# A ViT tower on one core: the tokenizer's loops written out, the image load behind a unit's first doubling, token tiles evacuated in two slots, an earlier meeting of the engines

## What is computed

```python
x = (x - mean) / (1e-06 + std); x = x / math.sqrt(P)          # per patch and channel
x = _conv2d(x, conv1_w, conv1_b)                               # 3x3, 3 -> 64 channels
residual = x
x = gelu(_group_norm(x, gn1_g, gn1_b)); x = _conv2d(x, rconv1_w, rconv1_b)   # 3x3, 64 -> 64
x = gelu(_group_norm(x, gn2_g, gn2_b)); x = _conv2d(x, rconv2_w, rconv2_b)   # 3x3, 64 -> 64
x = residual + x
x = _conv2d(x, proj_w, proj_b, stride=P, pad=0)                # one token of 192 per patch
embeddings = x.reshape(bsz, seq_len, E) + row_emb[row_pos][None] + col_emb[col_pos][None]
```

## Time and profile before

| what | us |
|---|---|
| median of 3 runs (lowest, highest) | 1486.84 (1485.9, 1489.83) |
| the profiled execution, its run's time | 1486.23 |
| its span in the trace | 1484.4 |
| PE busy in it | 1367.0 (92%) |
| DVE, ACT, POOL busy | 1098.0, 860.0, 582.6 |
| PE's mean granted clock | 0.98 of full speed |

### The profile page before, as it was taken

How to read it: one execution, slowest core, us unless ns; L and a number is a source line. 1 busy time by engine, 2 the same in 40 slices (tenths; PEclk the granted TensorE clock), 3 DMA queues, 4 the chain that set the end, 5 groups by cost and what they waited for, 6 DMA issues and landing times. The chain is left out here.

```text
span 1484.4 us, 43767 instructions
## 1 busy us (share of the span) xinstructions
PE 1367.0 (92%) x14042; PEld 1005.5 (68%) x14042; DVE 1098.0 (74%) x4148; ACT 860.0 (58%) x2126; POOL 582.6 (39%) x1116
## 2 busy tenths in 40 slices
PE   3999988888999999999999998999999977998889
PEld 1865543334888588768977875789588867754647
DVE  4763358999888988888898888888888864545520
ACT  1333337777767776666776766676767630343451
POOL 1000035555554544455455444455454420152600
PEclk9999999999999999999999999999999988898999
DMA  7899845544555555455545554555455579300000
GB/s 209 237 270 267 242 117 160 179 123 128 147 140 134 138 139 147 119 137 146 140 118 156 136 146 104 146 147 139 123 149 139 145 219 259 79 1 1 2 0 17
DMA packets 125141, 205.78 MB, mean 139 GB/s; under 512 B 20028, under 2 KB 88188, under 8 KB 124478
## 3 DMA queue, kind: packets, MB, share of 16 engines
q1 hardware_dynamic: 124990, 203.71, 50.3%
HBM read 103.11 MB, written 20.70 MB: 83 GB/s over the span
## 5 line engine op out<-in xcount | busy, mean ns | idle before, releaser
L629 PE MATMUL rc<-sb_acts,sb_rwd 128*64 128x512 f16 x1764 | 561.5, 391 | 21.4 <-DMA sb_acts<-sb_hst 21.2
L630 PE MATMUL rc<-sb_acts,sb_rwd 128*64 128x512 f16 x1764 | 562.3, 392 | 0.0
L481 POOL TENSOR_TENSOR sb_tmp<-sb_mst,sb_half_neg 128x8 f32<-128x8 f32 x200 | 353.6, 1768 | 463.8 <-DVE sb_mst L956 463.8
L548 ACT ACTIVATE sb_f32q<-c,sb_gsh,sb_gsc 128x128 f32<-128x128 f32 x792 | 298.3, 458 | 274.5 <-POOL sb_gsh L491 274.5
L629 PE MATMUL rc<-sb_acts,sb_rwl 128*64 128x512 f16 x1176 | 362.6, 390 | 5.3 <-issue 5.3
L630 PE MATMUL rc<-sb_acts,sb_rwl 128*64 128x512 f16 x1176 | 362.0, 390 | 0.0
L720 PE MATMUL pj_st<-sb_wall_arena 128*64 128x384 f16 x1792 | 304.0, 333 | 6.6 <-DVE sb_wall_arena L975 6.6
L568 ACT ACTIVATE sb_g2f<-rc,sb_gsh,sb_gsc 128x128 f32<-128x128 f32 x784 | 297.3, 481 | 4.6 <-POOL sb_gsh L491 4.6
L724 PEld LDWEIGHTS pj_st<-sb_wall_arena 128*64 128x64 f16 x1792 | 220.9, 222 | 65.8
L724 PE MATMUL pj_st<-sb_wall_arena 128*64 128x192 f16 x1792 | 240.9, 245 | 0.0
L629 PEld LDWEIGHTS rc<-sb_acts,sb_rwd 128*64 128x64 f16 x1764 | 179.1, 110 | 84.2 <-DMA sb_acts<-sb_hst 33.2
(11 more groups left out here) (190 smaller groups left out, 1864.0 us busy)
## 6 DMA issues: line engine op xcount, KB each, us to landing
sb_acts<-sb_hst SPq DMA_DIRECT2D x792, 78.8 KB, 2.6
sb_im<-x_planes SPq DMA_DIRECT2D x202, 136.5 KB
sb_wall_arena<-w_lo SPq DMA_DIRECT2D x48, 528.0 KB, 3.8
sb_acts<-sb_hst SPq DMA_DIRECT2D x96, 162.0 KB, 3.2
sb_wall_arena<-w_lo SPq DMA_DIRECT2D x24, 480.0 KB, 3.7
sb_f32q<-in_proj SPq DMA_DIRECT2D x12, 576.0 KB, 4.6
sb_wall_arena<-in_proj SPq DMA_DIRECT2D x12, 576.0 KB, 4.6
w_lo<-sb_wall_arena SPq DMA_DIRECT2D x8, 768.0 KB, 3.7
```

The costliest lines, as they stand in the source:

```text
L481: ch.did(gp.tensor_tensor(t1, var, half_neg[:, :], ALU.pow))
L548: ins = nc.scalar.activation(g1f[:, q * Q + m, :], c1[q][:, m * HALF:(m + 1) * HALF], ACT.Gelu, bias=gsh[q][:, m:m + 1], scale=gsc[q][:, m ...
L629: nc.tensor.matmul(out[0:CH, :], w_odd, x_odd, start=(n == 0), stop=(n == 14))
L630: yield nc.tensor.matmul(out[CH:128, :], w_even, x_even, start=(n == 0), stop=(n == 14))
```

## The change

It has four parts, all in the front and its border to the tail. No arithmetic changes.

1. **Loops written out**: every `Fori` becomes a Python loop, so each engine's program is one straight line. PE's program grows from 3652 to 9933 rows in the listing, DVE's from 987 to 2857, ACT's from 328 to 792, POOL's from 283 to 1041. The rows for registers, compares and branches go.
2. **Image load between the doublings**: SP issues `double` for q = 0 first, then waits for `s_c1` and issues `load_im`, then `double` for q = 1.
3. **Token tiles in two slots**: `tokens` becomes `tokens_high` and `tokens_low`, which DVE runs at the ends of slots 0 and 1 of the following group, rather than both behind the last slot of the group that projected the tile. SP stores the tile behind the second unit of that following group, no longer behind the last unit of the group before it.
4. **Earlier meeting**: the store of the last tile, `load_patches(3)` and `load_tokens(2)` are moved from the end of SP's front program to the start of its tail program.

```diff
@@ over_groups, over_units
-            group(0, 0, True)
-            with eng.Fori(0, (GROUPS - 1) // 2) as i:
-                group(2 * i + 1, 1, False)
-                group(2 * i + 2, 0, False)
+            for g in range(GROUPS):
+                group(g, g % 2, g == 0)
...
-            with eng.Fori(1, GU // 2) as j:
+            for j in range(1, GU // 2):
                 pair(g * GU + 2 * j, j, False)
@@ SP, main stage
-            def store_tokens(lo):
-                sp.dma_start(emb[bass.ds(lo, 64), :], tok[0:64, :]).then_inc(s_emb, 16)
-                sp.dma_start(emb[bass.ds(lo + 64, G - 64), :], tok[128 - (G - 64):128, :]).then_inc(s_emb, 16)
+            def token_store(g):
+                sp.wait_ge(s_pjr, g + 1)
+                sh.store_tokens(sp, emb, (g - 1) * G)
...
+                        double(2 * u + 2, 1 - p, 0)
                         sp.wait_ge(s_c1, 2 * u + 5)
                         load_im(u + 3, 1 - p)
-                        double(2 * u + 2, 1 - p, 0)
                         double(2 * u + 3, 1 - p, 1)
...
                         if not first and 2 * j + p < NCH:
                             load_chunk(g, 2 * j + p)
-                if not first:
-                    sp.wait_ge(s_pjr, g + 1)
-                    store_tokens((g - 1) * G)
+                        if g > 1 and u == g * GU + 1:
+                            token_store(g - 1)
...
             over_groups(sp, group)
+            token_store(GROUPS - 1)
@@ SP, end of the front
             load_tokens(1)
             load_patches(2)
-            sp.wait_ge(s_pjr, GROUPS + 1)
-            store_tokens((GROUPS - 1) * G)
-            load_patches(3)
-            load_tokens(2)
@@ DVE, main stage
                     split1(k + 2, q, 1 - p, pair_at + 1)
+                    if g > 1 and u == g * GU:
+                        (tokens_high, tokens_low)[q](g - 2)
...
-            with dve.Fori(0, (GROUPS - 1) // 2) as i:
+            for i in range(0, (GROUPS - 1) // 2):
                 group(2 * i + 1, 1, False)
-                tokens(2 * i)
                 group(2 * i + 2, 0, False)
-                tokens(2 * i + 1)
+            tokens_high(GROUPS - 2)
+            tokens_low(GROUPS - 2)
@@ SP, start of the tail
+            sh.store_tokens(sp, emb, (GROUPS - 1) * G)
+            sh.load(sp, 3, xst, xs, d_xs)
+            sh.load(sp, 2, embt, emb, d_em)
             ld(hmask[:, :], a["hmask"])
```

More of the change, by code:

```diff
@@ L119, in take, with load, store_tokens @@
         return view
+    def load(self, sp, k, dst, src, done):
+        for parts, tiles, rows in tile_loads(k, src):
+            sp.dma_start(dst[parts, tiles, :], rows).then_inc(done[k], 16)
+    def store_tokens(self, sp, emb, lo):
+        sp.dma_start(emb[lo:lo + 64, :], self.tok[0:64, :]).then_inc(self.s_emb, 16)
+        sp.dma_start(emb[lo + 64:lo + G, :], self.tok[128 - (G - 64):128, :]).then_inc(self.s_emb, 16)
 def tile_loads(k, src):
@@ L436, in load_patches @@
             def load_patches(k):
-                for parts, tiles, rows in tile_loads(k, xs):
-                    sp.dma_start(sh.xst[parts, tiles, :], rows).then_inc(sh.d_xs[k], 16)
+                sh.load(sp, k, sh.xst, xs, sh.d_xs)
             def load_tokens(k):
-                for parts, tiles, rows in tile_loads(k, emb):
-                    sp.dma_start(sh.embt[parts, tiles, :], rows).then_inc(sh.d_em[k], 16)
+                sh.load(sp, k, sh.embt, emb, sh.d_em)
             sp.wait_ge(s_half, 1)
@@ L556, in _ @@
                 fold_step(0, p, True)
-            with act.Fori(1, FU // 2 - 1) as i:
+            for i in range(1, FU // 2 - 1):
                 for p in range(2):
@@ L594, in group @@
                 pair(g * GU, 0, first, True)
-                with act.Fori(1, GU // 2) as j:
+                for j in range(1, GU // 2):
                     pair(g * GU + 2 * j, j, False, False)
@@ L600, in _ @@
             act.wait_ge(s_wst, 16 * LOW_STORES)
-            with act.Fori(0, (GROUPS - 1) // 2) as i:
+            for i in range(0, (GROUPS - 1) // 2):
                 group(2 * i + 1, 1, False)
@@ L700, in _ @@
                 fold_step(0, p, True)
-            with pe.Fori(1, FU // 2 - 1) as i:
+            for i in range(1, FU // 2 - 1):
                 for p in range(2):
@@ L920, in _ @@
             ins.then_inc(s_padz, 1)
-            with dve.Fori(5, FU // 2 - 1) as i:
+            for i in range(5, FU // 2 - 1):
                 fold_pair(i)
@@ L1003, in group, with tokens_high @@
                 pair(g * GU, 0, first, True)
-                with dve.Fori(1, GU // 2) as j:
+                for j in range(1, GU // 2):
                     pair(g * GU + 2 * j, j, False, False)
-            def tokens(g):
+            def tokens_high(g):
                 dve.wait_ge(s_pj, g + 2)
@@ L1011, in tokens, with tokens_low @@
                 v.tensor_scalar(tok[:, :], pj[:, 0:E], 1.0 / WS, None, ALU.mult).then_inc(s_tkh, 1)
+            def tokens_low(g):
                 dve.wait_ge(s_tkh, g + 1)
@@ L1084, in _ @@
             ins.then_inc(s_tcd, 1)
-            tokens(GROUPS - 1)
+            tokens_high(GROUPS - 1)
+            tokens_low(GROUPS - 1)
 NH, HS = 12, 16
@@ L1093, with build_tail @@
 LOWEST = float(np.finfo(np.float32).min)
-def build_tail(nc, a, emb, sh, out):
+def build_tail(nc, a, emb, xs, sh, out):
     with ExitStack() as ctx:
@@ L1184, in _ @@
             sp.wait_ge(sh.s_emb, 32 * GROUPS + 32)
-            for parts, tiles, rows in tile_loads(NT // 2 - 1, emb):
-                sp.dma_start(embt[parts, tiles, :], rows).then_inc(d_em[NT // 2 - 1], 16)
+            sh.load(sp, 3, embt, emb, d_em)
             ld(qb[:, :], a["qkb"])
@@ L1676, in build_program @@
         build_front(nc, a, emb, xs, ts, sh)
-        build_tail(nc, a, emb, sh, out)
+        build_tail(nc, a, emb, xs, sh, out)
 def layout(inp):
```

## The result

The changed kernel takes 1496.2 us (median of 14 runs, 1489.56 to 1513.23), the kernel before 1488.0 us (14 runs, 1483.55 to 1491.8). The ratio is 1.0058, with a 95% interval of 1.0036 to 1.0080: slower by some 8 us. The slowest of the 14 runs of the changed kernel (1513.23) counts as a slow execution and is left out of the ratio. The forecast was 1484.6, in a range from 1470 to 1493, and no change that can be told. Both its time and its range missed. The profiled execution of the changed kernel is its second fastest (1489.8 us, a span of 1487.8), so its trace shows less of the loss than most runs have.

What follows compares the result with a forecast made beforehand. PE was taken as the bound, busy 1367.0 of 1484.4 us; -6.6 + 0.7 + 12 - 4 - 1 - 3.2 = -2.1 gave a span of 1482.3 and a time of 1484.6 us, 8 in 10 from 1470 to 1493.

Steps and rivals of the forecast that it cites:

- loops: Outer back-edges: PE's idleness at two taken branches and the low clock after go, -6.6 us, bounds -5.3 and -8.
- meeting: Front-to-tail barrier: without SP's six loads PE starts the tail sooner, next waiting for L452's data; -3.2 us, -1.5 to -5.
- tokens: Group borders: token tile's operations moved into two slots shorten a group's first six slots; -1 us, between -4 and +2.
- the load's place: Image load behind the first doublings lands just in time, so disturbances of SP's issues reach PE: +12 us, 0 to +20.
- doublings: Groups 1 to 6: first doublings no longer queue behind the image load, so waits inside the groups go: -4 us.
- 24 x 0.4 = 9.6: Image load: 24 units with lengthened SP issues at 0.4 us average each, 9.6 us of the +12.
- Rival B: Image load needs over 7.6 us in every unit, PE waits 0.3 us in all 84 projecting units: 1494 us, chance 0.13.
- Case A: Image load has room (6.2 to 6.8 us) or fetches stop disturbing SP: 1472.6 us, to 1479 at a half; chance 0.36.
- The inner loops: No gain where PE is the bound; group 0 held by the image load's cycle: +0.7 us, between -5 and +3.
- The landing: Image load's time from issue: 6.2 us from its rate, at most 8.5 from a doubling queued behind it; 7.2 taken.

Runs made afterwards that it cites:

- e3: The kernel before with every loop written out and nothing else: 1473.0 us, ratio 0.9894.
- e4: The kernel before with only the last token store and six loads moved behind the barrier: 1485.3 us, ratio 0.9975.
- e8: The changed kernel with the image load ahead of the first doublings and both token tile operations behind a group's last slot as before: 1468.9 us.
- e1: The changed kernel with the image load again ahead of a unit's first doublings: 1467.0 us, ratio 0.9853.
- e9: The kernel before with only the outer loops (pairs of groups) written out on every engine: 1471.1 us, ratio 0.9887.
- e10: The kernel before with the inner loops (units, fold steps) written out and the outer loops kept: 1495.3 us, ratio 1.0042.
- e6: The changed kernel with the image load's first DMA ahead of the first doublings and its second behind them: 1453.4 us, ratio 0.9763.
- e7: The changed kernel with the image load issued by ACT, behind the first GELU of a unit's slot 0: 1474.8 us, ratio 0.9914.
- e5: The changed kernel with the image load between the second and third of the first four doublings: 1649.3 us, ratio 1.108.

## Why the prediction was wrong

The parts as measured add up: loops -16 (e3), meeting -4 (e4), tokens -2 or nothing (e8), the load's place +29 (changed less e1). That is +7 to +9, and +8 was measured.

- **The load's place** was forecast at +12, less 4 for doublings: +8. It cost 29, and 34 on the kernel before. The geometry was right: the load is issued 2.89 us behind the split in an undisturbed unit (2.96 forecast) and lands 7.02 us after that (7.2). PE waits for it, in units that a fetch disturbs, and the waits for doublings go. The step that failed is the price of a disturbance, the 0.4 us a unit in "24 x 0.4 = 9.6". I had taken 0.75 us of issue, less slack, and a landing that stays the same. In the 82 units counted above the 19 with a lengthened issue (0.82 us more) also have the load land later (7.52 against 7.02 us): both add up, 17.8 us of stall in 15 of them, 0.94 a unit. The 63 others have 5.1 us in 7, where 2 to 3 were forecast. Two terms were missing besides: group 0's 10.4 us of waits for the load, booked as +0.7, and the clock, which costs 5.1 us more than in e1, which the prediction had itself read at the back-edges and then left out here. In all, 33.6 us of waits stand where 12 were forecast. Against them, 17.1 us of waits for doublings go that e1 has, where 5 were taken off.
- **Rival B** came closest (1494, by a load that needs over 7.6 us and misses every unit), and it was close by luck, with the wrong mechanism: the stalls are 23 in groups 1 to 6, up to 2.7 us long, not 0.3 us in each of 84 units. Case A's chance of 0.36 was too high: by the prediction's own numbers the load had 0.1 us of slack (half of the undisturbed units had 0.4 or less), and a disturbance can only make it later.
- **The loops** were forecast at -6.6 + 0.7 and gave -16, all by the outer ones. In e3 the stretches with the two branches shorten by 4.5 and 6.3 us (groups 3 and 5 in the table), 10.8 where I had counted 6.6: two slots behind each branch stands one lengthened by a wait for a doubling (5.51 and 7.49 us before) that I had booked to the tokens. Such a slot is not tied to the branch alone: e9's trace, without the branch, still has one of 7.23 us at the start of group 3, with a wait of 2.1 us for a doubling. Groups 1, 2, 4 and 6 gained 5.5 us together. One cause is an error in my account of the kernel: I wrote that SP's program was written out. Its inner loops were, its outer loop was not, as the REGISTER_ALU rows in the listing of its queue show, and a load's two issues took 1.80 us with an address from a register against 1.52 in e9. The two issues of a load take 0.3 us less without it, and the doublings behind them can go out sooner: waits for doublings in the groups are 8.9 us in e9, 12.8 before.
- **The inner loops** at +0.7: right that they buy nothing where PE is the bound and that group 0 stays where the load's cycle puts it (132.9 us; 131.6 before). Wrong that they are free (e10).
- **The meeting** was forecast at -3.2, with `in_b` next: 3.7 in e4, and `in_b` it is.
- **Doublings**: 5 us were forecast to go in groups 1 to 6. All went, 12.8 us there and 8.4 in group 0. Without the late load they would stand at 17.1 us (e1).
- **The landing** of doublings was read from the kernel before as an upper bound for the load, 8.5 us. By the load's own completions in the trace it took 7.46 us in that unit, and 7.6 on average in the kernel before.
- **The range** ended at 1493 and the median is 1496.2. It was built from one execution; the changed kernel's own runs spread over more than 20 us.

What stays open: why the clock in the tail is lower in the changed kernel's trace (0.92) than in e1's (0.95), which run the same code and differ by 3.8 us there; how far the split of the traced 26 us holds for the slower executions of the changed kernel, up to 20 us above the traced one, of which no trace exists; by what way a fetch lengthens SP's issues; and why a load behind a lengthened issue lands 0.5 us later, since a fetch during its own flight makes no difference (7.01 us with one, 7.04 without, in undisturbed units).

## What to carry to other kernels

Before a transfer is moved to help another, write down for both when they are issued, when they are needed and what stands behind them; one with no slack left pays for the disturbances that it used to absorb, and one that is long and on few DMA engines delays what follows it on them, here from either queue. Where it can be split, one half in each place keeps slack for both (e6: -43 us against the changed kernel). Take apart an edit that gains and one that loses before judging either: three parts here were worth 22 us, the fourth cost 29.

## What was unexpected of the hardware

- A small DMA waits for a large one issued ahead of it even from another engine's queue: 4.4 us instead of 2.1 to landing (e7).
- A small DMA of 16 shares behind a long one of three is late on three of its shares only: 12 of the 64 completions of four doublings come last (53 of 82 sets before), 6 where two of the four stand behind the load (69 of 71 sets in e5).
- A set of four DMA issues took 3.21 us instead of 2.39 in 19 of 82 units, and in all 19 a fetch of 16 KB on q8 began within it; the load behind landed in 7.52 us instead of 7.02.
- Writing the inner loops out slowed the kernel by 6 us or more as long as the outer loop stayed (e10), while the outer loop alone, taken twice and on every engine, cost 16 (e9).
- After 1.92 us without work PE ran at the lower clock level for most of 2.6 us, which nearly doubled the price of this stall; of the 33 stalls for the load three had such a sequel.
